# Third chunk of k turned by PE in two fp16 parts, and the third quarter of M made of three fp16 products

## What is computed

```python
q = softmax(Wq @ layernorm(x), over the 64 features of a head) * 64 ** -0.5
k = softmax(Wk @ ctx, over the 1024 tokens)
v = Wv @ ctx
context = k @ v.T                        # for each head, 64 x 64
out = Wo @ (context.T @ q) + bo          # 128 x 1024
x = x + out / max(norm(out over channels), 1e-12) * g * sqrt(128)
x = x + layernorm(x) @ w + bias          # w: 1024 x 1024, 4-bit weights with scales and zeros
```

## Time and profile before

| | |
|---|---|
| median of 3 runs | 633.75 us (632.51 to 635.59) |
| the profiled execution | 635.1 us |
| its span in the trace | 633.3 us |
| mean granted TensorE clock | 0.987 |
| PE, PEld busy | 94%, 60% |
| DVE, ACT, POOL busy | 86%, 80%, 87% |
| chain of work that ended last | PE 74%, DVE 9%, ACT 5%, issue 4%, DMA 3%, POOL 3% |

### The profile page before, as it was taken

One profiled execution on the slowest core, in us unless ns is written; L12 is line 12 of the kernel. 1 busy time (PEld: TensorE's weight loads), 2 busy tenths in 40 slices (PEclk: granted clock), 3 DMA queues, 4 the chain that ended last, 5 costly groups with the idle time before them and its releaser, 6 DMA issues.

```text
span 633.3 us, 10844 instructions
## 1 busy us (share of the span) xinstructions
PE 596.1 (94%) x3431; PEld 380.6 (60%) x3447; DVE 543.2 (86%) x904; ACT 507.1 (80%) x789; POOL 548.9 (87%) x473
## 2 busy tenths in 40 slices
PE   4686799999999999999999999999999999998897
PEld 3454375656657575665657566665756666574654
DVE  4897789898988999888988988898898989889754
ACT  4888789797879879787988979797897978788442
POOL 4268879999999999999999999999899999999630
PEclk9888799999999999999999999999999999999999
DMA  9416658868596876868887885868698595848551
GB/s 324 108 36 147 120 140 152 208 97 208 116 151 184 157 189 129 187 125 171 167 138 184 142 202 117 179 143 141 182 152 198 121 194 116 154 116 162 111 141 67
DMA packets 246969, 96.19 MB, mean 152 GB/s; under 512 B 236136, under 2 KB 237952, under 8 KB 246912
## 3 DMA queue, kind: packets, MB, share of 16 engines
q1 hardware_dynamic: 240576, 72.42, 59.3%
q10 hardware_dynamic: 6336, 23.07, 10.7%
HBM read 28.85 MB, written 8.39 MB: 59 GB/s over the span
## 4 chain that ended last, share of the span: by engine, by line
PE 74%; DVE 9%; ACT 5%; issue 4%; DMA 3%; POOL 3%; SPq 1%; ACTq 0%; POOLq 0%; DVEq 0%
PE ps_m L1619 14%; PE ps_m L1493 7%; PE ps_k L1411 4%; PE ps_o L1503 4%; PE ps_o L1411 4%; PE ps_o L1412 4%; PE ps_o L1413 4%; PE ps_k L1413 4%; PE ps_k L1412 4%; PE ps_q L1411 3%; PE ps_q L1413 3%; PE ps_q L1412 3%; PE ps_ta L1472 2%; PE ps_o L1527 2%; PE ps_tb L1472 2%
## 5 line engine op out<-in xcount | busy, mean ns | idle before, releaser
L514 POOL TENSOR_TENSOR q_tok_lo<-q_exp,q_tok_hi 128x1024 f16<-128x1024 f32 x64 | 135.8, 2132 | 8.1 <-ACT q_tok_hi L748 7.3
L737 ACT ACTIVATE q_exp<-q_exp,w_unit 128x512 f32<-128x512 f32 x128 | 92.9, 726 | 53.4 <-DVE q_exp L1070 53.3
L486 POOL TENSOR_TENSOR q_exp<-q_exp,q_rec 128x1024 f32<-128x1024 f32 x63 | 119.9, 1904 | 4.9
L1065 DVE TENSOR_REDUCE q_nmax<-ps_q 128x8 f32<-128x512 f32 x128 | 86.9, 679 | 28.5 <-PE ps_q L1413 28.2
L1619 PE MATMUL ps_m<-w_int,x_parts 128*128 128x512 f16 x432 | 100.0, 379 | 0.3 <-DMA x_parts<-spare 0.2
L1070 DVE TENSOR_TENSOR q_exp<-ps_q,q_nmax 128x512 f32<-128x512 f32 x128 | 88.5, 692 | 4.4
L522 POOL TENSOR_TENSOR k_lo<-k_exp,k_hi 128x1024 f16<-128x1024 f32 x32 | 82.2, 2569 | 9.2 <-ACT k_hi L678 9.2
L1056 DVE TENSOR_REDUCE k_nmax<-ps_k 128x1 f32<-128x1024 f32 x64 | 77.1, 1205 | 5.2 <-PE ps_k L1413 4.9
L1493 PE MATMUL ps_m<-k_t,c_t 128*128 128x256 f32 x256 | 77.0, 383 | 0.0
L1077 DVE TENSOR_REDUCE q_sum<-q_exp 128x16 f32<-128x1024 f32 x64 | 76.9, 1201 | 0.0
L748 ACT ACTIVATE q_tok_hi<-q_exp 128x1024 f16<-128x1024 f32 x64 | 67.5, 1054 | 7.8 <-POOL q_exp L486 5.4
(11 more groups left out here) (221 smaller groups left out, 1461.7 us busy)
## 6 DMA issues: line engine op xcount, KB each, us to landing
x_res<-in_x ACTq DMA_DIRECT2D x16, 512.0 KB, 3.6
out_x<-y SPq DMA_DIRECT2D x15, 512.0 KB, 2.9
x_in<-in_x ACTq DMA_DIRECT2D x14, 512.0 KB, 4.8
c_in<-in_ctx ACTq DMA_DIRECT2D x14, 512.0 KB, 6.0
x_in<-in_x SPq DMA_DIRECT2D x2, 512.0 KB, 5.6
c_in<-in_ctx SPq DMA_DIRECT2D x2, 512.0 KB, 7.0
q_hi<-q_tok_hi SPq DMA_TRANSPOSE x64, 3.3
q_lo<-q_tok_lo SPq DMA_TRANSPOSE x64, 3.3
```

Of the source, the lines that this page charges most:

```text
L486: nc.gpsimd.tensor_tensor(pair, pair, rec.unsqueeze(2).to_broadcast([P, 2 * HEADS, DH]), ALU.mult).then_inc(qs_done, 1)
L514: nc.gpsimd.tensor_tensor(q_tok_lo[p % 2][:], q_exp[:, 2 * p:2 * p + 2, :].rearrange("p t d -> p (t d)"), q_tok_hi[p % 2][:], ALU.subtract ...
L737: nc.scalar.activation(q_exp[:, j, :], q_exp[:, j, :], ACT.Exp, scale=w_unit[:]).then_inc(qexp_done, 1)
L1065: nc.vector.tensor_reduce(q_nmax[:, j, :], heads, op=ALU.max, axis=AX_X, negate=True).then_inc(qmax_done, 1)
```

## The change

The third chunk of k is treated as the first two in precision, but not in how it is turned. ACT adds the bias to its maximum too (PARTED = 3 in place of TURNED). PE turns it in fp32 as before, ACT writes the copy of `ps_ta` and `ps_tb` in fp16 into a third part of `k_t_hi`, and DVE subtracts this from the same bank in a new call, `low_tk`, and writes the fp16 low part into `k_t_lo`. `transpose_k(2)` and `(3)` wait for that too, since they write the same banks. In `mix_m` the three fp16 products have 384 columns, and the fp32 product has 128. On DVE, `low_tk(0)` and `low_tk(1)` stand behind `scale_y(0)`, in pass 0 behind the last `pick_nibbles`; and `scale_y(1)` goes behind `shift_q(5)`.

```diff
 TURNED = 2
+PARTED = 3
...
-        k_t_hi = sb("k_t_hi", [P, TC, TURNED * P], F16)
-        k_t_lo = sb("k_t_lo", [P, TC, TURNED * P], F16)
-        k_t = sb("k_t", [P, TC, HID - TURNED * P])
+        k_t_hi = sb("k_t_hi", [P, TC, PARTED * P], F16)
+        k_t_lo = sb("k_t_lo", [P, TC, PARTED * P], F16)
+        k_t = sb("k_t", [P, TC, HID - PARTED * P])
...
         TK = 2 * (HC - TURNED)
+        TS = 2 * (PARTED - TURNED)
...
                 def exp_k(b, sums, j):
...
-                    if j < TURNED:
+                    if j < PARTED:
...
-                        act.wait_ge(kbias_done, TURNED * b + j + 1)
+                        act.wait_ge(kbias_done, PARTED * b + j + 1)
...
                     if k == 0 and begun(a):
                         act.wait_ge(m_ready, a)
-                    nc.scalar.activation(k_t[:, t0:t0 + 4, fc * P:(fc + 1) * P],
+                    to = k_t_hi if TURNED + fc < PARTED else k_t
+                    fc = fc + TURNED if TURNED + fc < PARTED else fc + TURNED - PARTED
+                    nc.scalar.activation(to[:, t0:t0 + 4, fc * P:(fc + 1) * P],
...
+                def low_tk(k):
+
+                    t0, fc = 4 * (k % 2), TURNED + k // 2
+                    dve.wait_ge(tk_moved, TK * a + k + 1)
+                    if k == 0 and begun(a):
+                        dve.wait_ge(m_ready, a)
+                    part = (slice(None), slice(t0, t0 + 4), slice(fc * P, (fc + 1) * P))
+                    nc.vector.tensor_tensor(k_t_lo[part], (ps_ta, ps_tb)[k % 2][:].rearrange("p (t c) -> p t c", t=4),
+                                            k_t_hi[part], ALU.subtract).then_inc(tklo_done, 1)
...
                     pick_nibbles(2)
                     pick_nibbles(3)
+                    low_tk(0)
+                    low_tk(1)
                     shift_q(3)
...
                     scale_y(0)
+                low_tk(0)
+                low_tk(1)
                 if do_n:
                     abs_c()
                 shift_q(4)
                 invert_k()
                 sum_q(a, 1)
+                shift_q(5)
                 if do_f and i != END:
                     scale_y(1)
-                shift_q(5)
...
                         pe.wait_ge(tk_moved, TK * a + k - 1)
+                        pe.wait_ge(tklo_done, TS * a + k - 1)
...
                         pe.wait_ge(tk_moved, TK * (a + 1))
+                        pe.wait_ge(tklo_done, TS * (a + 1))
...
                     for t in range(t0, t1):
-                        three(ps_m[:, 0:TURNED * P], c_t_hi[s][:, t, :], c_t_lo[s][:, t, :], k_t_hi[:, t, :],
+                        three(ps_m[:, 0:PARTED * P], c_t_hi[s][:, t, :], c_t_lo[s][:, t, :], k_t_hi[:, t, :],
                               k_t_lo[:, t, :], start=(t == 0), stop=False)
-                        last = nc.tensor.matmul(ps_m[:, TURNED * P:], c_t[s][:, t, :], k_t[:, t, :], start=False,
+                        last = nc.tensor.matmul(ps_m[:, PARTED * P:], c_t[s][:, t, :], k_t[:, t, :], start=False,
                                                 stop=(t == TC - 1))
```

More of the change, by code:

```diff
@@ L140, in build @@
         k_lift = sb("k_lift", [P, 1])
-        k_bias = sb("k_bias", [P, TURNED])
+        k_bias = sb("k_bias", [P, PARTED])
         k_hi = [sb(f"k_hi{j}", [P, N], F16) for j in range(TURNED)]
         k_lo = [sb(f"k_lo{j}", [P, N], F16) for j in range(TURNED)]
-        k_t_hi = sb("k_t_hi", [P, TC, TURNED * P], F16)
-        k_t_lo = sb("k_t_lo", [P, TC, TURNED * P], F16)
-        k_t = sb("k_t", [P, TC, HID - TURNED * P])
+        k_t_hi = sb("k_t_hi", [P, TC, PARTED * P], F16)
+        k_t_lo = sb("k_t_lo", [P, TC, PARTED * P], F16)
+        k_t = sb("k_t", [P, TC, HID - PARTED * P])
         q_tok_hi = [sb(f"q_tok_hi{r}", [P, 2 * HID], F16) for r in range(2)]
@@ L252, in build @@
         tk_moved = sem("tk_moved")
+        tklo_done = sem("tklo_done")
         tc_ready = sem("tc_ready")
@@ L1053, in max_k @@
                         dve.wait_ge(kexp_done, 4 * (b - 1) + j + 1)
-                    if begun(b) and j < TURNED:
-                        dve.wait_ge(kbias_done, TURNED * (b - 1) + j + 1)
+                    if begun(b) and j < PARTED:
+                        dve.wait_ge(kbias_done, PARTED * (b - 1) + j + 1)
                     nc.vector.tensor_reduce(k_nmax[:, j:j + 1], ps_k[:], op=ALU.max, axis=AX_X,
```

## The result

The changed kernel takes 657.79 us (median of 6 runs, 655.56 to 661.70) where the kernel before takes 633.90 (6 runs): 1.038 times the time, 95% interval 1.035 to 1.041, or 23.9 us more. The forecast was 658.0, with a range of 648 to 670. The profiled executions are 635.1 us before and 655.56 after, 20.4 us apart in their spans (633.3 and 653.7); that one of after is the shortest of its six runs.

What follows compares the result with a forecast made beforehand. PE was taken to bound the kernel, with 0.18 us slack in a pass. Thirteen full passes at 1.69 + 0.12 - 0.20 give 20.9 us, the other passes 3.0: 24 us more, median 658, range 648 to 670.

Steps and rivals of the forecast that it cites:

- The bound: Full passes: PE is busy 36.13 of 36.31 us, so losses beyond 0.18 us can't be made up in the pass.
- The M product: mix_m on PE: 0.715 us a chunk in place of 0.77, 0.44 us less in a pass.
- What of it arrives: At m_t after mix_m: 0.20 of the 0.44 us saved arrives, since m_t then waits for ACT's last exponential of k.
- The stall: At transpose_k(2): PE waits for low_tk(0), queued on DVE behind scale_y(0); 1.69 us lost in a pass.
- The bias: At project_k(3): exp_k(2) waits for one more ACT instruction, so PE loses 0.12 us in a pass.
- Full passes: The 13 passes i = 2 to 14: 13 x (1.69 + 0.12 - 0.20) = 20.9 us more.
- The other passes: Passes 0, 1 and 15: 1.6, 1.1 and 0.3 us more, 3.0 together.
- (c): Rival at transpose_k(2): DVE has the low part ready in time, the stall vanishes, not slower, 632 us; chance 0.03.
- (d): Rival in mix_m: M's product gets no shorter, 3 us more, 661 us; inside the range, counted with the forecast's 0.78.
- (b): Rival: stall partly repaid, by all 0.44 us arriving or cheaper fp32 products, and a free bias; 646 us; chance 0.08.
- (a): Rival: the stall at transpose_k(2) brings PE's clock down, 1.6 us more each time, 668 to 679 us; chance 0.11.

Runs made afterwards that it cites:

- e1: Changed kernel with DVE's low_tk(0) moved right after shift_q(2) and low_tk(1) after shift_q(3), both ahead of scale_y(0): 642.58 us, 1.013 times the kernel before.
- e4: Changed kernel with two more DVE instructions of the same form ahead of the first low part, from pass 2 on: 696.33 us, 1.098 times the kernel before.
- e6: Changed kernel with scale_y(1) put back ahead of shift_q(5), as in the kernel before: 657.34 us.
- e7: Changed kernel, reordered: project_q(4) ahead of transpose_k(2), transpose_k(3) inside the second feed-forward product, low_tk(0) ahead of scale_y(0), abs_c behind shift_q(4): 640.63 us, 1.008.
- e8: Changed kernel with one more DVE instruction of the same form ahead of the first low part, from pass 2 on: 680.94 us, 1.072 times the kernel before.
- e3: Changed kernel without low_tk and PE's waits for it, third part of k_t_lo left zero: 635.98 us, 1.003 times the kernel before.
- e10: Order of e7, without the third chunk's bias, last x2 statistics instruction (bn_aggr) behind max_k: 638.94 us, 1.008 times the kernel before.

## Why the prediction was right

**The bound.** PE had 0.18 us to spare in a pass, and nothing of the new idle time was made up later. That step carried the rest, and the two kernels with the wait alone and the products alone show it: the parts add up to the whole (36.12 + 1.66 = 37.78).

**The M product.** 0.715 us a chunk was forecast. The timeline of PE of after, answering to the earlier trace rows:

```profile
352.22 0.33 PE L1430 MATMUL ps_m<-k_t_hi,c_t_lo 128*128 128x384 f16 x1
...
352.71 0.38 PE L1514 MATMUL ps_m<-k_t,c_t 128*128 128x128 f32 x2
352.93 0.33 PE L1430 MATMUL ps_m<-k_t_hi,c_t_lo 128*128 128x384 f16 x1
```

0.49 for the fp16 products, 0.22 for the fp32 one, 0.71 together. The narrow fp32 instruction takes 0.11 us, as in the row with full weights, and not the 0.068. It is also half of what the instruction of 256 columns took (0.22), so this row doesn't tell whether its weight load or its columns set it. By the rule of the Trainium skill for a weight load (TensorE: Matmul & The Clock Gate, section LDWEIGHTS (loading the stationary operand)) 128 columns take about 107 ns, an estimate worked out from it; it excludes the 0.068 as well, and the measured 0.11 agrees.

**What of it arrives.** 0.20 was forecast, 0.30 is measured. ACT at the end of mix_m, answering to the earlier trace rows:

```profile
358.56 0.19 ACT L673 ACTIVATION_READ_ACCUMULATOR k_exp<-ps_k,k_bias 128x1 f32 x1
358.65 0.68 ACT L786 ACTIVATE m_t<-ps_m,g_fit 128x512 f32<-128x512 f32 x1
```

m_t waits for ACT and no more for PE, as forecast. But an instruction of ACT starts 0.1 us before the shown end of the one ahead: I had taken 347.63, the end, as the earliest start, and it is 347.53. A term of 0.10 us, mis-sized in 13 passes: 1.3 us.

**The stall.** 1.69 forecast, 1.66 measured, from three rows: the start of DVE's next instruction, the duration of a like one and the wake-up.

**The bias.** 0.12 forecast, 0.13 by the run without it.

**Full passes.** 13 x 1.61 = 20.9 forecast, 18.4 found. 1.3 of it is the term above. Another 1.3: the full passes before weren't all 36.31; the longer ones, up to 36.99 from one mix_g to the next, add up to 1.3 us over the shortest, and after the change all but the first lie within 0.03 us of 37.78. I had left them out of the sum.

**The other passes.** 3.0 forecast. In the profiled pair +1.35 (pass 0), -0.85 (pass 1), +0.54 (pass 15) and +0.95 behind it, 2.0 together. Pass 1 is wrong in its sign: the stall of 2.55 us at its transpose_k(2) is there, but less of the stretch runs at the low clock (mean 0.94 from 64 to 94 us, and 0.89 before). Since after lay 24 us above before in the medians and 20.4 in the profiled pair, the right median is in part luck, a balance: full passes over-counted by 2.5 us, and a difference between runs of some 3 us. The profiled pair is a long run of before (635.1 beside a median of 633.9) and the shortest of after. That pass 0 can make such a difference is shown by the experiments whose pass 0 is that of the changed kernel (e1, e4, e6, e7, e8): up to the first mix_g their profiled executions took 53.34, 52.40, 53.01, 53.27 and 57.97 us, at mean clocks of 0.97 to 0.82, where the changed kernel's took 51.57 at 0.93. So one execution of each kernel doesn't check the 1.6 us forecast for pass 0.

**The rivals.** (c) and (d) didn't come: the written order of DVE held, and the products have their new shapes. (b) came for 0.10 of its 0.24 us in m_t. (a) didn't come, but stood nearer than the 0.11 I gave it says: the clock falls in seven of thirteen passes with one DVE instruction more in the stall. I had also read its two examples from windows. The timeline of before gives the whole idle times, 1.74 us with the clock left at 1.00 and 2.22 us with the fall:

```profile
53.05 0.49 PE L1411 MATMUL ps_k<-c_hi,wk_lo 128*128 128x512 f32 x1 [1.74 <-ACT k_exp L670]
...
57.60 0.80 PE L1411 MATMUL ps_k<-c_hi,wk_lo 128*128 128x512 f32 x1 [2.22 <-ACT k_exp L670]
```

The new idle of 1.47 us lay below both, not between them.

## What to carry to other kernels

Price a new wait by what stands ahead of the awaited instruction on its own engine, and not by that instruction's length alone: here 0.7 us of work cost 1.66 us in a pass, because it stood behind an instruction that itself waited for PE's last product. Before such a wait goes in, look for a place where the producer is ahead of the consumer, or give the waiting engine other work there: both orders tried here took nearly all of the loss away (36.39 and 36.23 us in a pass, beside 36.12 without the low part). And where the bounding engine has no slack, check what the saved time runs into next (here 0.30 of 0.44 us arrived), and price the passes that are not full by themselves. Read the granted clock of each timed run beside its time before a few us are put down to an edit.

## What the runs showed of the hardware

In these three kernels a stall that repeats in each pass brought the clock from 2.4 to 1.2 GHz in none of the thirteen passes at 1.47 us of idle time, in seven at 2.07 and in twelve at 2.67, and each fall cost 1.7 us. At 2.07 us, from pass 2 on, every second pass fell. Passes between the two kinds weren't seen, as was expected before e8 ran.

What stays open: the kernels with shorter full passes than before (36.12 in e3, 36.23 in e7, 35.99 in e10) were not faster in the medians. e7 and e10 were 5.7 and 4.0 us slower, where passes 2 to 14 of their profiled executions sum to 1.2 and 3.4 us less than before; e1 was 8.5 us slower, where they sum to 1.7 us more. Less granted clock in the timed runs goes with most of this, and leaving pass 0 alone brought clock and time back to nearly those of the kernel before. In the profiled executions of e1, e7 and e10 the clock was at 1.00 from pass 2 to pass 14, and below it mainly in passes 0 and 1. Whether the timed runs, which have no trace, lose it at the same place wasn't shown, nor why.
